# Transposing DMAs in place of TensorE transposes and ScalarE copies in the first block of a two-block transformer kernel

## The reference, cut to what matters

```python
def act_quant(x):
    s = 127.0 / jnp.clip(jnp.max(jnp.abs(x), axis=-1, keepdims=True), EPS)
    return jnp.clip(jnp.round(x * s), -128, 127) / s

# first block (B=8, T=512, D=512, 16 heads, hidden 2048)
xn = adaln(x, c, g1, w_ada1, b_ada1)
q, k, v = bitlinear(xn, w_qkv, b_qkv)            # bitlinear(x, w, b) = act_quant(x) @ ternary(w).T + b
o = softmax(q @ k.T * 32 ** -0.5) @ v            # per head
x = x + bitlinear(o, w_proj, b_proj)
xn = adaln(x, c, g2, w_ada2, b_ada2)
x = x + bitlinear(gelu(bitlinear(xn, w_fc1, b_fc1)), w_fc2, b_fc2)
# second block: RMS norm, FiLM, one-head attention, projection, MLP of 2048, all in fp32
```

## Time and profile before

| what | value |
|---|---|
| median of 3 executions | 2235.45 us (2235.22 to 2237.21) |
| span of the profiled execution | 2237.3 us |
| its own time | not listed apart from the span; the highest of the three, 2237.21 us, lies 0.1 us from it |
| TensorE busy with matmuls | 1987.5 us, 89% of the span |
| VectorE, ScalarE, GpSimd busy | 68%, 51%, 35% |
| mean granted TensorE clock | 0.978 of full speed |
| DMA engines, mean | 90 GB/s; the SP queue's packets took 23.4% of 16 engines' span |

### The profile page before, as it was taken

One profiled execution on the slowest core, in us unless ns is written; L12 is line 12 of the kernel. 1 busy time (PEld: TensorE's weight loads), 2 busy tenths in 40 slices (PEclk: granted clock), 3 DMA queues, 4 the chain that ended last, 5 costly groups with the idle time before them and its releaser, 6 DMA issues.

```text
span 2237.3 us, 40636 instructions
## 1 busy us (share of the span) xinstructions
PE 1987.5 (89%) x13326; PEld 1003.8 (45%) x13503; DVE 1530.2 (68%) x2667; ACT 1144.3 (51%) x2090; POOL 772.1 (35%) x705
## 2 busy tenths in 40 slices
PE   4787878899989998899989998899989998899889
PEld 3354334544444444544444444544444444544434
DVE  5676657875688657875688757875788757875422
ACT  4575644754465543844466443844456443744230
POOL 2173433641255113640255113740255103741021
PEclk8899999999999999999999999999999999999989
DMA  8443533021311123031411123021321123021212
GB/s 303 144 172 109 201 127 99 26 104 62 129 49 58 67 96 99 26 104 62 128 49 58 67 96 99 26 104 53 118 68 53 72 96 99 26 71 44 94 38 94
DMA packets 85529, 200.87 MB, mean 90 GB/s; under 512 B 7612, under 2 KB 48864, under 8 KB 73144
## 3 DMA queue, kind: packets, MB, share of 16 engines
q1 hardware_dynamic: 77528, 174.88, 23.4%
q10 hardware_dynamic: 7776, 23.10, 2.8%
HBM read 161.97 MB, written 35.72 MB: 88 GB/s over the span
## 4 chain that ended last, share of the span: by engine, by line
PE 42%; issue 28%; POOL 17%; DVE 7%; ACT 5%; DMA 0%; POOLq 0%; ACTq 0%; SPq 0%; DVEq 0%
POOL memory L1257 12%; PE banks L1435 8%; PE banks L1434 8%; PE banks L1436 8%; PE banks L1327 5%; PE banks L1392 5%; DVE memory L1012 2%; PE banks L1309 1%; POOL memory L1004 1%; PE banks L1378 1%; POOL memory L1180 1%; ACT memory L1045 1%; POOL memory L1474 1%; DVE memory L1019 1%; DVE memory L1027 1%
## 5 line engine op out<-in xcount | busy, mean ns | idle before, releaser
L1435 PE MATMUL banks<-memory 128*128 128x512 bf16 x1512 | 574.2, 380 | 19.5 <-DVE memory L1506 6.6
L1434 PE MATMUL banks<-memory 128*128 128x512 bf16 x1438 | 550.4, 383 | 23.1 <-DVE memory L1559 7.8
L1436 PE MATMUL banks<-memory 128*128 128x512 bf16 x1491 | 566.4, 380 | 1.3
L1257 POOL TENSOR_TENSOR memory<-memory 128x512 bf16<-128x512 f32 x332 | 375.7, 1152 | 366.5 <-ACT memory L1246 365.2
L1246 ACT ACTIVATE memory<-banks 128x512 f32<-128x512 f32 x512 | 290.9, 599 | 129.6 <-PE banks L1239 127.2
L1660 POOL TENSOR_TENSOR memory<-memory 128x512 bf16<-128x512 f32 x128 | 144.7, 1132 | 487.6 <-DVE memory L1655 487.6
L1189 PE MATMUL banks<-memory 96*128 96x512 bf16 x512 | 186.7, 392 | 73.6 <-DVE memory L1201 39.1
L1434 PEld LDWEIGHTS banks<-memory 128*128 128x128 bf16 x1536 | 149.0, 97 | 217.1 <-issue 15.5
L1201 DVE TENSOR_REDUCE memory<-banks 128x1 f32<-128x512 f32 x320 | 207.8, 680 | 37.6 <-PE banks L1189 37.4
L1436 PEld LDWEIGHTS banks<-memory 128*128 128x128 bf16 x1536 | 148.5, 97 | 186.7 <-issue 4.3
L1435 PEld LDWEIGHTS banks<-memory 128*128 128x128 bf16 x1536 | 152.1, 99 | 165.4 <-issue 3.8
(11 more groups left out here) (176 smaller groups left out, 2951.2 us busy)
## 6 DMA issues: line engine op xcount, KB each, us to landing
memory<-weight_parts SPq DMA_DIRECT2D x80, 1024.0 KB, 4.9
memory<-head_parts SPq DMA_DIRECT2D x192, 128.0 KB, 2.8
head_parts<-memory SPq DMA_DIRECT2D x64, 256.0 KB, 2.8
memory<-in_x SPq DMA_DIRECT2D x32, 256.0 KB, 3.3
memory<-ada_rows SPq DMA_DIRECT2D x16, 512.0 KB, 4.5
memory<-in_L_cond_w_fc ACTq DMA_DIRECT2D x2, 4096.0 KB, 14.3
memory<-in_L_cond_mlp_w SPq DMA_DIRECT2D x8, 1024.0 KB, 7.7
weight_parts<-memory SPq DMA_DIRECT2D x8, 1024.0 KB, 4.9
```

The lines of the kernel that those rows point to most:

```text
L1257: eng.tensor_tensor(prob_lo[:, e % RING], expo[:, e % RING], prob_hi[:, e % RING], ALU.subtract).then_inc(ok.sem, 1)
L1434: pe.matmul(bank, lh, rh, start=(k == 0), stop=False)
L1435: pe.matmul(bank, lh, rl, start=False, stop=False)
L1436: mm = pe.matmul(bank, ll, rh, start=False, stop=(k == KC - 1))
```

## The change

The integers are turned by `dma_start_transpose`, bf16, SBUF to SBUF, issued from SP. TensorE's turn_xq and turn_hidden and ScalarE's copy_xq and copy_hidden are gone, with their bank slots. Users of xq wait for the DMA's semaphore, and whole0 and whole_hidden wait for it before they overwrite what it reads. There is one DMA per 128x512 tile of xq (12 per sample) and one per 128x2048 tile of hid_int (4 per sample), written to two buffers in turn (hid_q and the space of qk_f). The pieces' stores and loads in `both(0, None)`, which stood together, are spread between the hidden turns.

```diff
@@ block0_jobs @@
-    for t in range(TT):
-        general(("xq", 0, t))
...
-            jobs.extend((("hT", t - 1, n), 4 + n % 2) for n in range(4))
-            jobs.append((("fc2", t - 1), 4))
+            jobs.append((("fc2", t - 1), 4 + t % 2))
@@ two_blocks @@
+        top[0] += -top[0] % 8
+        hid_turned = (hid_q, qk_f.rearrange("p a n -> p (a n)").bitcast(BF16).rearrange("p (f n) -> p f n", f=FC))
+        xq_in = [signal(f"xq_in{t}", 3 * 16) for t in range(TT)]
+        hid_in = [signal(f"hid_in{h}", TT // 2 * 16) for h in range(2)]
...
                 if c > 0:
-                    ready(dve, plan0, ("xq", c - 1, t), i)
+                    dve.wait_ge(xq_in[t].sem, xq_in[t](i, 16 * c))
...
+        def turn_xq(sp, i, c):
             for t in range(TT):
+                sp.wait_ge(y_int_ok.sem, y_int_ok(i, c * TT + t + 1))
+                sp.sem_inc(turn_begins, 1)
+                sp.dma_start_transpose(xq[:, :, t * P:(t + 1) * P], y_int[:, t]).then_inc(xq_in[t].sem, 16)
+
+        def xq_ready(pe, i, c, tiles):
+            for t in tiles:
+                pe.wait_ge(xq_in[t].sem, xq_in[t](i, 16 * (c + 1)))
...
         def qk_product(pe, i, c, parts="qk"):
             if c == 0:
-                all_done(pe, plan0, [("xq", 0, t) for t in range(TT)], i, ("q", 0))
+                xq_ready(pe, i, 0, range(TT))
...
         def proj0(pe, i):
             for t in range(TT):
-                all_done(pe, plan0, [("xq", 1, t)], i, ("proj", t))
+                xq_ready(pe, i, 1, (t,))
...
         def fc1_0(pe, i, t):
-            all_done(pe, plan0, [("xq", 2, t)], i, ("fc1", t, 0))
+            xq_ready(pe, i, 2, (t,))
...
+        def turn_hidden(sp, i, t):
+
+            sp.wait_ge(h_int_ok.sem, h_int_ok(i, t + 1))
+            sp.sem_inc(turn_begins, 1)
+            sp.dma_start_transpose(hid_turned[t % 2], hid_int).then_inc(hid_in[t % 2].sem, 16)
...
         def fc2_0(pe, i, t):
-            all_done(pe, plan0, [("hT", t, n) for n in range(4)], i, ("fc2", t))
+            pe.wait_ge(hid_in[t % 2].sem, hid_in[t % 2](i, 16 * (t // 2 + 1)))
...
@@ SyncE: both @@
+PIECES_AT = ((0, 1, 2), (3, 4), (5,), (6, 7))
                 units(j, 2, 3)
                 if i is not None:
+                    turn_xq(sp, i, 0)
...
-                units(j, 4, 6)
+                units(j, 4, 5)
                 if j is None:
                     done(sp, plan0, ("o", H - 1), i)
                     for n in range(3):
                         load_piece(sp, n)
+                if i is not None:
+                    turn_xq(sp, i, 1)
+                units(j, 5, 6)
                 if ahead:
                     done(sp, plan0, ("proj", TT - 1), i)
                     load_x(sp, x_d[1:B], i)
                     sp.wait_ge(y_full.sem, y_full(i, 2 * TT))
                     load_ada(sp, ada_d[1:B], i, 0)
-                if j is None:
-                    for n in range(N_PIECES):
-                        store_piece(sp, n)
-                        if n + 3 < N_PIECES:
-                            load_piece(sp, n + 3)
-                units(j, 6, N_UNITS)
+                if i is not None:
+                    turn_xq(sp, i, 2)
+                units(j, 6, 8)
+                if i is not None:
+                    for t in range(TT):
+                        turn_hidden(sp, i, t)
+                        if j is None:
+                            move_pieces(sp, PIECES_AT[t])
+                        if t in (1, 2):
+                            units(j, 7 + t, 8 + t)
+                else:
+                    units(j, 8, N_UNITS)
```

More of the change, by code:

```diff
@@ L27 @@
 STACK = 3 * HD
-MEMORY = 53184
+MEMORY = 53192
 N_BIAS = 36
@@ L202, in block0_jobs @@
     for t in range(TT):
-        general(("xq", 1, t))
-    for t in range(TT):
         general(("proj", t))
-    for t in range(TT):
-        general(("xq", 2, t))
     for t in range(TT + 1):
@@ L1051, in whole0 @@
                 if c > 0:
-                    ready(dve, plan0, ("xq", c - 1, t), i)
+                    dve.wait_ge(xq_in[t].sem, xq_in[t](i, 16 * c))
                 dve.tensor_scalar(y_int[:, t], y[:, t], MAGIC, None,
                                   ALU.subtract).then_inc(y_int_ok.sem, 1)
-        def turn_xq(pe, i, c):
+        def turn_xq(sp, i, c):
             for t in range(TT):
[L1058 to L1067, removed]
+                sp.wait_ge(y_int_ok.sem, y_int_ok(i, c * TT + t + 1))
[4 more added lines that the diff above has]
+                pe.wait_ge(xq_in[t].sem, xq_in[t](i, 16 * (c + 1)))
         def diagonals(dve, i):
@@ L1368, in whole_hidden @@
             if t > 0:
-                ready(dve, plan0, ("hT", t - 1, 3), i)
+                dve.wait_ge(hid_in[(t - 1) % 2].sem, hid_in[(t - 1) % 2](i, 16 * ((t - 1) // 2 + 1)))
             dve.tensor_scalar(hid_int, hid, MAGIC, None, ALU.subtract).then_inc(h_int_ok.sem, 1)
[L1372 to L1384, removed]
+        def turn_hidden(sp, i, t):
+            sp.wait_ge(h_int_ok.sem, h_int_ok(i, t + 1))
+            sp.sem_inc(turn_begins, 1)
+            sp.dma_start_transpose(hid_turned[t % 2], hid_int).then_inc(hid_in[t % 2].sem, 16)
         def fc2_0(pe, i, t):
-            all_done(pe, plan0, [("hT", t, n) for n in range(4)], i, ("fc2", t))
+            pe.wait_ge(hid_in[t % 2].sem, hid_in[t % 2](i, 16 * (t // 2 + 1)))
             b = take(pe, plan0, ("fc2", t), i)
@@ L1391, in fc2_0 @@
                 for f in range(4 * n, 4 * n + 4):
-                    mm = pe.matmul(banks[:, b], hid_q[:, f], w0_fc2[:, f], start=(f == 0), stop=(f == FC - 1))
+                    mm = pe.matmul(banks[:, b], hid_turned[t % 2][:, f], w0_fc2[:, f], start=(f == 0), stop=(f == FC - 1))
             mm.then_inc(full[b].sem, 1)
@@ L1719, in units, with move_pieces @@
                         load_unit(sp, j, n)
+            def move_pieces(sp, pieces_now):
+                for n in pieces_now:
+                    store_piece(sp, n)
+                    if n + 3 < N_PIECES:
+                        load_piece(sp, n + 3)
             def both(i, j, ahead):
@@ L1960, in both @@
                 highs1(j, M[ACT_CUTS[3]:14])
-                if i is not None:
-                    copy_xq(act, i, 2)
                 join(j, "copy")
                 for t, (m0, m1, m2, m3) in enumerate(CUTS):
-                    if i is not None and t > 0:
-                        copy_hidden(act, i, t - 1, (0, 1))
                     if i is not None and t < TT:
                         gelu0(act, i, t)
-                    highs1(j, M[m0:m1])
-                    if i is not None and t > 0:
-                        copy_hidden(act, i, t - 1, (2, 3))
-                    highs1(j, M[m1:m2])
+                    highs1(j, M[m0:m2])
                     if i is not None and t < TT:
@@ L2293, in both @@
                 join(j, "turn")
-                if i is not None:
-                    turn_xq(pe, i, 2)
                 if j is None:
@@ L2301, in both @@
                     for t in range(1, TT + 1):
-                        turn_hidden(pe, i, t - 1, range(4))
                         if t + 1 < TT:
@@ L2309, in both @@
                         fc1_0(pe, i, t)
-                    if i is not None and t > 0:
-                        turn_hidden(pe, i, t - 1, (0, 1))
-                    products1(j, M[m0:m1])
-                    if i is not None and t > 0:
-                        turn_hidden(pe, i, t - 1, (2, 3))
-                    products1(j, M[m1:m2])
+                    products1(j, M[m0:m2])
                     if i is not None and t > 0:
```

5 lines of the change are left out of this document (1 added, 4 removed).

## The result

The changed kernel took 2249.6 us (median of 12 runs) against 2237.8 us of the kernel before (12 runs): ratio 1.0043, 95% interval 1.0031 to 1.0055. (A ratio here is not the quotient of the two medians, which is 1.0053; the two measures differ by up to 0.001.) It is slower by about 10 us, and 2214 was forecast. The twelve runs lie in two groups, four at 2242 to 2244 us and eight at 2249 to 2253; the profiled one is of the upper group, and why there are two stays open. The profiled execution spans 2249.7 us (before 2237.3) and took 2251.5 by its own time.

A forecast was written before the change was run, and what follows sets the result against it. TensorE was taken to bound the MLP part (busy 67.6 of 68.0 us). Per pass 3.5 - 0.8 + 0.7 + 0.2 + 0 = 3.6 us, seven passes 25, less 4: 21 saved, about 2214 us as a median; range 2188 to 2296.

The forecast's parts named there:

- 3.5 us of identity products a pass, all on the path: MLP part: removing 8 groups of 0.44 us of hidden-row turning from TensorE saves 3.5 us per pass.
- Lx = 3.0, Lh = 5.5: Time in us from issue to landing of one transposing DMA: Lx for 128 KB xq tiles, Lh for 512 KB hidden tiles.
- Hidden waits -0.8: MLP part: TensorE waits 0.8 us per pass for the turn of hidden tile 0, nothing for the other tiles.
- c = 2, gain 0.7: Turns before fc1: fc1_0 can start at 988.7 instead of 989.42, gaining 0.7 of 1.6 us per pass.
- c = 1, gain 0.2: Turns before proj0: proj0 starts at 967.5 instead of 967.72, gaining 0.2 us per pass.
- SP's queue: Order of turns and loads on SP, which issues the DMAs: claimed to cost nothing in a loop pass.
- c = 0, nothing: Turns before qk_product: no gain, as TensorE waits for VectorE's diagonals; no loss, as the DMA has 4.5 us of cover.
- First pass +4, between 0 and 8: First pass: 2 us lost at c = 1, 2 at c = 0, piece 3's hold mostly hidden; together +4 us.
- Rival B: DMA waits replace identity products, with slower turns: +7 us a pass, 8 in the first, about 2293 us; chance 0.31 with beyond.
- rival A: Turns as fast as plain transfers, wholly hidden: 6.2 us gained a pass, no first-pass loss, 2192 us; chance 0.15.

## Why the prediction was wrong, by its own steps

- **3.5 us of identity products a pass, all on the path:** right. The MLP part lost 3.7, and the hidden rows alone gave 23 us of 24.5.
- **Lx = 3.0, Lh = 5.5:** too high; 2.3 and 3.7. The packets under 512 B grew from 7612 to 126396, by 118784, and 96 turns of 512 pieces and 32 of 2048 are 114688, so the pieces are nearly as I counted them; what was wrong is their price. 128 pieces per engine at 0.050 us would be 6.4, and the whole tile landed in 3.7. The Trainium skill (Advanced Engine Details and Errata, X-Bar Transpose) says that transposing DMAs are as fast as plain ones on this chip; the trace agrees as far as it can tell, 3.7 us against 4.6 for the ada rows of the same size, which come from DRAM. Its 1309 ns for a square (VectorE: DVE Perf Modes, "The three transpose paths") isn't a price per square in a larger transfer: sixteen landed in 3.7 us, 0.23 each.
- **Hidden waits -0.8:** none in the loop. The turn of tile 0 was issued at 1277.07 and fc2_0 started at 1282.36 without a wait.
- **c = 2, gain 0.7:** nearly right. fc1_0 waited 0.42 us and started 0.6 us after the products ahead of it (1264.52 and 1265.10), where it was 1.6: 1.0 a pass. The whole time tells less: the step is -4 us over the loop, within its noise, and the passes differ by 0.4 us, 3 in all; 5 were forecast.
- **c = 1, gain 0.2:** failed, -1.7 in the changed kernel's own passes. Two steps. I worked with the transfer's length and not with its issue: a turn takes 1.2 us of SP, so the tiles come 1.33 us apart while proj0 wants one every 0.9, and proj0 is 1.2 us longer (4.87 us from its start to the next product, 3.67 before). "SP's queue" was searched for what stands behind the turns, never for the turns themselves. And the cover was read off the kernel before, where the first tile was ready 1.6 us ahead of the end of the products (964.5 and 966.12). In the changed kernel it was 0.5 (1240.36 and 1240.86). The kernel before with the 8-byte shift alone lost the same microsecond, so it is the shift that shrank the cover; I had no term for it.
- **c = 0, nothing:** failed, -1.7 in six passes of seven and -0.6 in the seventh. "Nothing, because the wait is for the diagonals" is right for the wait and wrong for the clock: the identity products that cost nothing kept TensorE busy, and without them the granted clock fell to 0.67 in those six. This was named nowhere, not even among the rivals. The 4.5 us of cover for the DMA was cut to less than nothing by SP's pace as well, and showed as soon as the clock was held.
- **First pass +4, between 0 and 8:** failed, 13 us by the runs. c = 0 was put at 2 us and cost 9: its turns took up to 14 us to land beside the loads of the ScalarE queue. For the hold of piece 3 I had 5 us hidden by VectorE's joins; ScalarE was idle for 12 us and gelu stood behind it, 7 us net for the hidden rows and the pieces' places together. c = 1, where I put the other 2, cost nothing that can be told.

The sum by the runs: -23 - 4 + 12 + 11 + 13 = +9 us, and 10 were measured. The steps were cut from one chain of ratios, so that they add up is no proof of them; the proof is in the stretches of the traces. Rival B, slower, came nearest in its places: 1.6 us between tiles (1.33 were seen), losses of 2.2 at c = 0 and 2.7 at c = 1 (1.7 each), 8 in the first pass (13). Its reason, Lx near 4, didn't happen, and its hidden loss neither; the transfers were rival A's. What decided was in neither: issue time, clock, the 8-byte shift, and the order of one pass that isn't like the others.

Spreading the turns at c = 1 over two queues was not tried, nor one DMA for its four tiles. The Trainium skill (Advanced Engine Details and Errata, X-Bar Transpose) forbids two streams of transposes in flight at a time, and no run here shows it.

## What to carry to other kernels

Take to a transposing DMA what has microseconds of cover and is large: the hidden rows, one issue for sixteen squares, paid in full, while the four small turns at c = 0 and c = 1, which TensorE waits for at once, lost more than they saved in the kernels that were run. Before calling a removed instruction free because its engine would only have waited, ask what that wait does to TensorE's clock. Before blaming the change itself, run the kernel before with the shift of memory alone and compare the stretches, not only the time: slack that costs nothing today may be what the change lives on. And price a DMA three times: its landing, its issue on the queue's engine, and its neighbours in the one pass that moves the weights.

## What the runs showed that was not expected

- The issue of a transposing DMA holds SP for 1.2 us (128x512) or 1.6 us (128x2048), and they land in 2.3 and 3.7 us when the engines are free, in up to 14.0 us beside bulk loads.
- A pause of 1.87 us, where before there were identity products, was followed in six passes of seven by a granted clock of 0.67 over the next 5.25 us (matmuls at half speed for 4 us of them), and in the seventh by 1.00; two kernels with the same turns in the loop had the fall in three and in two of seven. Filling it with unused products, with nothing else changed, kept it at 1.00 in all seven and gave 0.0018 of the ratio, and with the turn made ready in time 0.0048.
- An 8-byte shift of the activations against the bias rows makes GpSimd's 128x512 f32 additions 16% slower (1092 to 1272 ns), and in the same kernel VectorE starts its integers at c = 1 1.0 us later against TensorE.
